# Layer 1's weighted rows shared six to two between ScalarE and VectorE, with another order of the scatters, the fill and the weights

## The reference

```
x = x + cross_attention0(layernorm(x), ctx)   # 8 heads of 8 channels, rope, output projection
x = x + experts0(layernorm(x))                # 64 experts, the best 8 of each token
x = x + cross_attention1(layernorm(x), ctx)   # no rope, no output projection
x = x + experts1(layernorm(x))                # the best 8, at most 128 rows of an expert in a block of 512 tokens
```

## Time and profile before

| what | value |
|---|---|
| median of 3 runs | 2177.61 us (2177.58, 2177.61, 2186.87) |
| the profiled execution's own time | 2174.09 us |
| its span | 2172.4 us |
| mean granted TensorE clock | 0.940 |
| busy: PE, DVE, ACT, POOL | 1717.8 (79%), 1454.2 (67%), 1261.7 (58%), 973.4 (45%) us |
| layer 0, last scatter starts | 681.25 us |
| layer 0's experts, first transpose | 697.12 us |
| layer 1, first gather | 1168.30 us |
| layer 1, first exponential | 1236.83 us |

### The profile page before, as it was taken

One profiled execution on the slowest core, in us unless ns is written; L12 is line 12 of the kernel. 1 busy time (PEld: TensorE's weight loads), 2 busy tenths in 40 slices (PEclk: granted clock), 3 DMA queues, 4 the chain that ended last, 5 costly groups with the idle time before them and its releaser, 6 DMA issues. The chain is left out here.

```text
span 2172.4 us, 45251 instructions
## 1 busy us (share of the span) xinstructions
PE 1717.8 (79%) x12879; PEld 1131.3 (52%) x12879; DVE 1454.2 (67%) x4556; ACT 1261.7 (58%) x3268; POOL 973.4 (45%) x1114
## 2 busy tenths in 40 slices
PE   4999999898972999999995487887887778856551
PEld 2555555555542788898884134444444444534440
DVE  5888888888853445555434478988998989843331
ACT  1777776666751566666664367777776767732210
POOL 4266666666654000000003655555555554138883
PEclk9999999999995999999997599999999999968996
DMA  5678877777634976666664677886767665358856
GB/s 146 150 210 232 216 198 196 194 203 196 185 103 148 342 226 199 198 201 198 197 192 137 171 169 190 199 204 172 178 174 171 173 169 152 79 146 190 187 94 111
DMA packets 413088, 390.98 MB, mean 180 GB/s; under 512 B 46640, under 2 KB 385072, under 8 KB 412848
## 3 DMA queue, kind: packets, MB, share of 16 engines
q1 hardware_dynamic: 341888, 259.97, 45.2%
q0 software_dynamic: 37904, 90.22, 16.7%
q10 hardware_dynamic: 33056, 37.90, 6.0%
HBM read 233.74 MB, written 170.16 MB: 186 GB/s over the span
## 5 line engine op out<-in xcount | busy, mean ns | idle before, releaser
L851 ACT ACTIVATE prob<-psE 128x512 f32<-128x512 f32 x1024 | 603.2, 597 | 319.1 <-PE psE L1427 267.9
L1042 DVE TENSOR_REDUCE mx<-psS 128x2 f32<-128x512 f32 x1024 | 682.5, 674 | 121.8 <-PE psS L1416 111.4
L710 POOL DMA_INDIRECT yg<-y_d,row_all x256 | 257.6, 1006 | 646.9 <-SPq L373 486.1
L1427 PE MATMUL psE<-q,k 128*128 128x256 bf16 x2048 | 398.3, 277 | 43.7 <-ACT prob L851 37.8
L1416 PE MATMUL psS<-k,q 128*128 128x512 bf16 x1024 | 399.7, 392 | 18.6 <-DMA k<-k_stack_d 8.9
L1532 PE MATMUL psE<-wt,xgT 128*128 (+1 forms) x1536 | 325.3, 335 | 1.2 <-ACT xgT L943 1.0
L1368 DVE TENSOR_TENSOR hid<-sil,psE 128x96 f32<-128x96 f32 x384 | 97.5, 254 | 335.4 <-ACT sil L948 310.4
L698 POOL DMA_INDIRECT xs_d<-xr,posi x256 | 251.3, 982 | 127.0 <-ACT prob L851 79.2
L1427 PEld LDWEIGHTS psE<-q,k 128*128 128x128 bf16 x2048 | 182.9, 99 | 235.5 <-ACT prob L851 97.8
L1443 PE MATMUL psO<-prob,v 128*32 128x256 f32 x4096 | 278.0, 389 | 9.4 <-ACT osb L832 9.4
L943 ACT COPY xgT<-psS 128x256 f32<-128x256 f32 x384 | 144.5, 376 | 205.5 <-PE psS L1526 143.1
(11 more groups left out here) (217 smaller groups left out, 2682.8 us busy)
## 6 DMA issues: line engine op xcount, KB each, us to landing
xg<-xs_d SPq DMA_DIRECT2D x320, 128.0 KB, 2.6
y_d<-y_all SPq DMA_DIRECT2D x320, 128.0 KB, 2.4
q<-q_stack_d SPq DMA_DIRECT2D x128, 256.0 KB
k<-k_stack_d SPq DMA_DIRECT2D x128, 256.0 KB
wt<-in_gu ACTq DMA_DIRECT2D x128, 192.0 KB
q_stack_d<-parts SPq DMA_DIRECT2D x64, 192.0 KB
k_stack_d<-parts SPq DMA_DIRECT2D x64, 192.0 KB
wt<-in_dn ACTq DMA_DIRECT2D x128, 96.0 KB
```

Source lines behind the costliest of these rows:

```text
L710: g.indirect_dma_start(yg[:, k, :], None, y0_d[:, :], bass.IndirectOffsetOnAxis(row_all[:, row(st.pair("load") * K + k, 1)], 0))\
L851: a.activation(prob[gr][:, u % 4, :], psE[ring][:, :], ACT.Exp, scale=SCALE).then_inc(s_exp, 1)
L1042: v_.tensor_reduce(mx[b][:, bg // 4, :].rearrange("p (h r) -> p h r", h=2)[:, :, (bg % 4) * 2 + tt], psS[(UNITS * (st.s0 - LAG["smax"]) + ...
L1427: ins = m_.matmul(psE[ring][:, i * T:(i + 1) * T], k2[b][:, bg, hh * T + i * P:hh * T + (i + 1) * P], q2[b][:, bg, :], start=True, stop=True)
```

## The change

Six parts, with no part of the computation left out:

- Layer 0: scatters 0 to 4 of a pair are issued in the step of place, 5 to 7 in that of post. They read the row numbers from `row_all`, which DVE writes at unit 5; the separate `posi` copy at unit 8 goes.
- Both layers: at slot s, PE waits for the weights of group s/8 - 1, and so for none ahead of slot 0.
- SP reads the table of first rows ahead of the barrier in front of layer 0's experts.
- Layer 1's fill: a step gathers rows 0 to 4 of its pair at its end, and 5 to 7 behind the roots of the next step. The sums of the early pairs, and Q, qk and the parts of the step numbered 4, move to late units.
- Layer 1's sum: ACT multiplies six rows (units 0, 1, 2, 3, 5, 7), DVE two (units 4, 6). DVE adds two by two (unit 5), once more 512 wide and once 256 wide (unit 8), and into x2 (unit 9). The moments of x2 come at units 10 and 11 of the same step.
- Layer 1's order: gathers are paced at units 2 to 9; the route's xr and xT, the parts and hote's product on ACT come one unit earlier, as does XT on PE; DVE's hotr goes from unit 7 to unit 0 of its step, and rankf from unit 10 to 13.

```
+PACE = ((6, 8, 10, 12, 14, 0, 2, 4), (2, 3, 4, 5, 6, 7, 8, 9))
+AT_ONCE = 5
+FULL = 6
+BY_ACT = 6
+PRODUCTS = (0, 1, 2, 3, 5, 7)
+ADDED, TWO, ONE, ALL, MOMENTS = (4, 6), (5, 8), 8, 9, (10, 11)
+AHEAD_OF_ROOTS = 5
...
-                if before and s % FB == 0 and s < E:
-                    before(s // FB)
+                if before and s % FB == 0 and 0 < s <= E:
+                    before(s // FB - 1)
...
                 def scatter(k, unit):
-                    if not st.on("post"):
+                    stage = "place" if k < AT_ONCE else "post"
+                    if not st.on(stage):
                         return
...
                 if L == 0:
-                    for k in (0, 1, 2, 3):
+                    for k in (5, 6, 7):
                         scatter(k, PACE[L][k])
+                    scatter(0, PACE[L][0])
                     rotated()
-                    for k in (4, 5):
+                    for k in (1, 2):
                         scatter(k, PACE[L][k])
                     remainder()
-                    scatter(6, PACE[L][6])
+                    scatter(3, PACE[L][3])
                     third_part()
-                    scatter(7, PACE[L][7])
-                elif st.on("attn"):
-                    for k in range(K):
-                        gather(k, PACE[L][k])
+                    scatter(4, PACE[L][4])
+                else:
+                    if 0 < st.s0 < FULL:
+                        for k in range(AHEAD_OF_ROOTS, K):
+                            gather(Step(1, st.s0 - 1), k, 0)
+                    if st.s0 >= FULL - 1:
+                        for k in range(K):
+                            gather(st, k, PACE[L][k])
                     remainder()
                     third_part()
-                else:
-                    remainder()
-                    third_part()
-                    for k in range(K):
-                        gather(k, PACE[L][k])
+                    if st.s0 < FULL - 1:
+                        for k in range(AHEAD_OF_ROOTS):
+                            gather(st, k, 0)
...
+                    if u == added[0]:
+                        add_row(st, 6)
+                    if u == two[0]:
+                        dve.wait_ge(s_comb, st.n1("comb", BY_ACT, 4))
+                        ch.add(v_.tensor_tensor(ys[:, 0:2, :], ys[:, 0:2, :], ys[:, 2:4, :], ALU.add), "two")
+                    if u == added[1]:
+                        add_row(st, 7)
+                    if u == two[1]:
+                        ch.join("two")
+                        dve.wait_ge(s_comb, st.n1("comb", BY_ACT))
+                        ch.add(v_.tensor_tensor(ys[:, 0:2, :], ys[:, 0:2, :], ys[:, 4:6, :], ALU.add), "four")
+                    if u == one:
+                        ch.join("four")
+                        ch.add(v_.tensor_tensor(ys[:, 0, :], ys[:, 0, :], ys[:, 1, :], ALU.add), "one")
+                    if u == all_:
+                        ch.join("one")
+                        dve.wait_ge(s_sum, st.n1("comb", 2))
+                        wait(dve, d_x2[b], st.nbuf1("comb") - 16)
+                        v_.tensor_tensor(x2[b][:, :], ys[:, 0, :], ys[:, 6, :], ALU.add).then_inc(s_x2, 1)
+                    if u == moments[0]:
+                        dve.wait_ge(s_x2, st.n1("comb"))
+                        ch.add(v_.bn_stats(stats[:, 0, :], x2[b][:, :]), "stats0")
+                    if u == moments[1]:
+                        if st.on("front") or st.on("route"):
+                            dve.wait_ge(s_rstd, 4 * st.roots())
...
-                    if u == 7 and st.on("post") and L == 1:
+                    if u == 0 and st.on("post") and L == 1:
+                        ch.join("rankf")
+                        wait(dve, s_lsp, st.n1("post", 1, 0))
                         v_.tensor_tensor(hotr[:, :, :], over_k(iota_r), over_e(rankf[:, 0, :], P), ALU.is_equal)\
                           .then_inc(s_lhs, 1)
```

More of the change, by code:

```diff
@@ L458, in nbuf0, with slots @@
                 return self.it * 16 + 16 * ((self.s0 - FLAG[stage]) // FB + 1 - back)
-        def slots(layer, body, look_up=None, before=None, aside=None):
+        def slots(layer, body, look_up=None, before=None, aside=None, table=None):
             end = JOBS[layer] + FLAG["D"]
-            table = {}
+            table = {} if table is None else table
             for s in range(end):
@@ L688, in scatter, with gather @@
                 def scatter(k, unit):
-                    if not st.on("post"):
+                    stage = "place" if k < AT_ONCE else "post"
+                    if not st.on(stage):
                         return
-                    b = st.buf("post")
+                    b = st.buf(stage)
                     if k == 0:
-                        hold(pool, s_posi, st.n1("post"))
-                        if st.s0 == LAG["post"] + PAIRS - 1:
+                        hold(pool, s_posi, st.n1(stage))
+                        if st.s0 == LAG[stage] + PAIRS - 1:
                             pool.wait_ge(d_zero, 16 * CLEARS)
-                    else:
-                        paced(unit)
-                    g.indirect_dma_start(xs_d[:, :], bass.IndirectOffsetOnAxis(posi[b][:, k:k + 1], 0),
+                    paced(unit)
+                    g.indirect_dma_start(xs_d[:, :], bass.IndirectOffsetOnAxis(row_all[:, row(st.pair(stage) * K + k, 1)], 0),
                                          xr[b][:, 0:T], None).then_inc(d_sent[b], 16)
-                def gather(k, unit):
+                def gather(st, k, unit):
                     if not st.on("load"):
@@ L839, in max_rows @@
                     a.copy(mhi[h][:, :], psM[item_bank(L, f"mT{h}")][0:16, 0:P]).then_inc(s_mhi[h], 1)
+                filled = L == 1 and st.s0 == FULL - 2
                 for u in range(UNITS):
@@ L881, in body @@
                         max_rows("attn", 1)
[L882 removed]
+                    if u == (10, 11)[L] and st.on("route"):
                         act.wait_ge(s_xtp, st.n("route"))
@@ L912, in body @@
                          .then_inc(s_v, 1)
-                    if u == 11 - L and st.on("front"):
+                    if u == (15 if filled else (11, 9)[L]) and st.on("front"):
                         b = st.buf("front")
@@ new lines, in sums @@
+                def sums(st, u):
+                    added, two, one, all_, moments = units_of_sum(st.s0)
+                    if not st.on("comb"):
+                        return
+                    b = st.buf("comb")
+                    if u == added[0]:
[23 more added lines that the diff above has]
+                            dve.wait_ge(s_rstd, 4 * st.roots())
+                        wait(dve, s_xn, last(st, "comb"))
+                        ch.join("stats0")
+                        v_.bn_aggr(mv[:, 0, :], stats[:, 0, :]).then_inc(s_mvx, 1)
@@ L1113, in body @@
                         split_max("smax", 0)
-                    if u == 10 and st.on("place") and L == 1:
+                    if u == 13 and st.on("place") and L == 1:
+                        wait(dve, s_lhs, st.n1("place", 1, 0))
                         ch.join("rank")
@@ L1129, in body @@
[L1129 to L1150, removed]
+                        v_.tensor_scalar(row_all[:, row(st.pair("place"), K)], chosen[b][:, :], -CHOSEN, None, ALU.add)\
+                          .then_inc(s_posi, 1)
@@ L1459, in product, with q_rows @@
                     ins.then_inc(done, 1)
+                def q_rows(st):
+                    b = st.buf("front")
+                    product("Q", "front", [(s_xn, st.n("front"))],
+                            [(wbd[L][n][:, :], xn[b][:, :]) for n in ("qr", "q")[L]], s_qp)
                 for u in range(UNITS):
```

100 lines of the change are left out of this document (62 added, 38 removed).

## The result

The changed kernel takes 2218.44 us (median of 4 runs, 2204.93 to 2228.25) against 2178.33 us for the kernel before: ratio 1.0165, 95% interval 1.0138 to 1.0192. By the ratio it is about 36 us slower, by the two medians 40. The forecast was 2176 within 2148 to 2194, and it was wrong. The profiled execution has a span of 2221.2 us, a little above its median.

What follows compares the result with a forecast made beforehand. Limits differ by stage: DVE is busiest in layer 1's steady attention (162 of 180 us), POOL in the experts at the end. Terms -6.3 - 1.4 - 2 + 8.4 = -1.3 gave 2176 us on the median's basis, range 2148 to 2194.

Steps and rivals of the forecast that it cites:

- Scatters, -6.3: End of layer 0's attention: five of a pair's eight scatters go one step earlier, so the last ends 6.3 us sooner.
- Weights, -1.4: Start of layer 0's experts: PE no longer waits for the second group's weights; ACT's first copy comes sooner, -1.4 us.
- Fill, -2: Fill of layer 1: gathers placed in POOL's waits ahead of rem save 2 us, between bounds 0 and -8.
- First half, +0.62: Layer 1's steady step, red 0 to nrm(0): hotr adds 1.21 us, the moments of x2 leave; sum +0.62.
- rival 2: ACT bounds the steady step's red 0 to nrm(0); xn up to 1.71 us later; 2194 us in all; chance 0.21.
- Window fixed at 3.76: Layer 1's steady step, nrm(0) to the ninth reduction (red 8): PE sets these 3.76 us, with hotr there or not.
- Rival 1: Steady step's stretch from nrm(0) to red 8 shrinks by up to 1.62 us: 2139, or 2158 with half; chance 0.33.
- Second half, -0.21: Layer 1's steady step, red 8 to next red 0: fewer additions, moments added, x2 clear of rem (-0.54); sum -0.21 us.
- the case that x2 itself stays beside rem: Layer 1's steady step: if x2 still met rem on the shared port, 0.54 us a step returns, some 13 us.
- the steady step: Layer 1's attention: summed to +0.41 us a step, taken as +0.35; over 24 steps +8.4 us.
- The steps at the ends: Layer 1's attention: steps 6 to 8 gain 0.8 us each, 33 to 36 lose up to 1.21 each; together 0.

Runs made afterwards that it cites:

- e4: Kernel before with only the change's layer 0 part (scatters, wait for weights, SP's table read): 2164.19 us, ratio 0.9955.
- e8: Kernel before with only the split of layer 1's rows, six weighted on ACT and two on DVE: 2186.4 us, ratio 1.0062.
- e1: Changed kernel with hotr alone back at unit 7: 2182.84 us, ratio 1.0062.
- e3: Kernel before with only hotr moved to unit 0 and rankf to unit 13: 2200.58 us, ratio 1.0133.
- e12: Changed kernel with old gather pace, hotr at unit 7, rankf at unit 10, and the op writing normalised weights at unit 13: 2152.59 us, ratio 0.9917.
- e2: Changed kernel with the DVE op that writes the normalised weights at unit 7, not 9, in layer 1: 2165.29 us, ratio 0.9975.
- e6: Changed kernel with only the old pace of layer 1's gathers restored: 2162.32 us, ratio 0.9955.
- e7: Changed kernel with the op that writes the normalised weights as a broadcast tensor_tensor, still at unit 9: 2213.59 us, ratio 1.0183.

## Why the prediction was wrong

- *Scatters, -6.3.* Right: 6.3 in the changed kernel and in e4, and DVE's table, at 677.84, now ends 2.2 us ahead of the last scatter (680.01), where the forecast left 1.6.
- *Weights, -1.4.* Wrong: ACT's first copy comes 1.5 us sooner, but the stage ends when it did (473.2 and 473.6 us against 473.5), and drain and experts together gain 6.4 in all the profiles, not 7.7. What takes it back within the stage I did not test.
- *Fill, -2.* Wrong: 69.7 us from first gather to first exponential against 68.5, and 67.1 to 69.7 in all the profiles with six rows and the new order, against 68.5 to 69.4 with four rows and the old one: no gain that stands out from their spread. The step that failed took ACT's later landing as a bound and not as a cost: e8 shows that six rows on ACT cost 7.7 us in the fill, and the new order only pays for that.
- *First half, +0.62.* The mechanism was right (e1, e3: hotr was hidden in the window and is not at unit 0), the size was not: 1.15. DVE's idle time ahead of nrm(0), whose rise I did not price, rose from 0.15 to 0.50 a step; that is 0.35 of the 0.53 that are missing. xn ended 1.6 us later after the step's first exponential (9.60 against 8.01), close to rival 2's 1.71. nrm(0) still ended after it (9.83), and Q starts 0.21 after nrm(0) as before (0.22), so xn did not yet decide. Rival 2, which alone had the kernel slower by more than 0.5% (2194), was right in the sign but not in what decides.
- *Window fixed at 3.76.* Wrong: it was 3.26 in the changed kernel and between 2.59 and 3.81 in the others. Rival 1 had this right in kind; it gave 0.55 of its 1.62. The early step of rows 8 showed only that hotr does not lengthen the window, and I read it as if nothing could. What sets it stays open.
- *Second half, -0.21.* **This is the step that failed most**, with +0.82. I wrote that x2 and rem part, and gained 0.54 for it. They did part (0.96 to 0.44). But I moved rem without asking what it meets in its new place. It meets the weight op, and third_part meets rankf at its new unit (0.17 to 0.36). What the weight op's place beside rem is worth, e12 shows with 17 us; e2 and e6, which take it away, win 41 and 46, but more than the op's own time moves in them. The prediction gave some 13 us to the case that x2 itself stays beside rem; that another op would take its place was in no rival.

Together the steady step gave +1.41 and not +0.35, over 24 steps 34 us against 8.4. The steps at the ends, which I had at 0 (-2.4 for the steps 6 to 8, up to +4.8 for 33 to 36), measured +7.7 and +0.3 in the two profiles; what the early ones lose was not tested. The loss is confined to layer 1's attention but for some 4 us in the experts after it (2221.15 - 1976.87 = 244.3 from the first gather to the end, against 2172.38 - 1932.23 = 240.2), which e1 to e4 do not show (240.6 to 241.7) and which I did not follow up.

## What to carry to other kernels

When an instruction of GpSimd with large SBUF inputs moves in time, go through VectorE's instructions at its new place as well as at its old one: who meets it changes, and a short op held for 1 to 1.8 us holds everything behind it. Read a short instruction's mean duration against its own in another stretch before pricing it; one of 0.25 us that shows 1 us is being held, in some of its executions or in all; its single durations tell which. A wait that hides work is a place to put work in, so before an op leaves it, price the op in full where it goes, with what the other engines lose by it.

## What the runs showed of the hardware

Three VectorE instructions of different forms were held beside GpSimd's subtraction rem (128x512 f32, 1.17 us). Their means are: an addition with two inputs in SBUF (x2), 0.96 us against 0.42; a tensor_scalar (the weight op), 0.96 to 1.23 in the changed kernel, e1 and e12 against 0.25; a conversion (rankf), 0.72 in e3 and 0.81 in e6 against 0.17. A tensor_tensor in the weight op's place took 1.85 (e7). The Trainium skill, SBUF — State Buffer, "Who interferes with whom", has VectorE and GpSimd share a port pair under an exclusive lock, with tensor_scalar, copies and casts able to take it in their two-port modes and two-input instructions against a GpSimd read; the rows agree with both groups. I had expected it only for the two-input one. In one point the recorded starts do not agree: by that section the instruction that issues first gets the pair, but the weight op starts 0.6 us ahead of rem (1506.17 and 1506.77) and ends with it all the same. Why stays open; GpSimd's spans are rough in this profile. The reductions, whose input is in PSUM, kept 0.67 us in all kernels.
